# Loading a batch's max queries after its second key third, and half B's query DMAs split over three batches

## The chip, the cores and the metric

The kernel runs on one core of a Trainium2 chip. The metric is the device time of one execution in microseconds (us), as the median of several executions. The profiled execution is one further execution, taken by the hardware profiler.

## The reference, cut to what matters

Four transformer-like blocks run one after the other on `x` (16 batches of 56 rows, 128 wide) with a context of 1500 rows in each batch. Blocks 1, 2 and 3 each have a cross attention with 16 heads of 8 dimensions from the 56 rows to the 1500 context rows. That attention is where the change lies:

```python
q = (xq @ Wq + bq).reshape(B, Lq, nh, dh)
kv = (xkv @ Wkv + bkv).reshape(B, Lkv, 2, nh, dh)
k = kv[:, :, 0]
v = kv[:, :, 1]
scores = jnp.einsum('bqhd,bkhd->bhqk', q, k) / jnp.sqrt(jnp.float32(dh))
attn = jax.nn.softmax(scores, axis=-1)
out = jnp.einsum('bhqk,bkhd->bqhd', attn, v).reshape(B, Lq, H)
return x_q + (out @ Wp + bp)
```

Block 0 and the self attentions of blocks 2 and 3 stand outside the change.

## The kernel before, in words

Every engine has its own hand-written program, and the engines meet at semaphores. One cross attention ("layer" 1, 2 or 3 in the code) goes through its 16 batches with one call of `attend` for each batch, on every engine. `attend` gets `batch` (b), `following` (b+1), `behind` (b+2) and `third` (b+3).

TensorE (PE) does four things in `attend(b)`, woven together over twelve slots c = 0 to 11. It computes the scores of batch b, chunk by chunk (L1395). It computes the score maxima's input for batch b+1 in 24 "units" (L1343, function `unit`): unit 0 stands at c = 0 right behind the first chunk of scores, units 8 and 16 follow at about c = 4 and c = 7. It multiplies probabilities by values (L1369). And it prepares batch b+2: transposes of the context (L1208) at c = 1 to 3, its keys in three thirds of 500 columns (L1213) at c = 4, 6 and 8, then its values (L1219). Since PE works in order, unit 0 of batch b+1 stands ahead of everything else of `attend(b)` but the first chunk of scores.

The keys take a long way. ScalarE (ACT) evacuates a third to `k_full` (L878); GpSimd (POOL) splits it into two fp16 parts `k_hi` and `k_lo` (L698, L700); SyncE (SP) stores both parts to DRAM (`k_out`, L527, two DMAs) and loads them back in another layout as the tile `k_st` (`k_in`, L539, six DMAs). `k_in` waits for the landing of `k_out`. SP issues all of these DMAs, in the order in which its program is written, and waits in that order too.

The queries of all batches of a layer lie in `q_all`, and SP copies those of one batch at a time into two double-buffered tiles: `q_mx` for the units (function `q_max`) and `q_st` for the scores (function `q_scores`), both through `q_for` (L564). `unit` waits at u = 0 for `q_mx` of its batch and for the first key third:

```python
if u == 0:
    pe.wait_ge(sem(f"q_mx_loaded{p}"), 16 * (B // 2 * cr["n"] + i + 1))
    ...
if u % NP == 0:
    pe.wait_ge(sem(f"k_stacked{t}"), STACKED * (n + 1))
```

`q_all` is filled in two halves of eight batches. Half A is done in `first`, ahead of the layer. Half B (batches 8 to 15) is made while batches 4 to 6 run: VectorE (DVE) finishes the split queries in `attend(4)` at c = 6 (L1814), SP writes them to DRAM (`q_out`, L546, two DMAs of 224 KB) and reads them back in stacked form (`q_stack`, L555, six DMAs of 112 KB), and `q_ready` waits for their landing. SPLIT_BATCH is 4.

`load` (L480) fetches the context of batch b+4; it waits until the transposes of batch b+2 are done.

Of the kernel before, what the change touches and what calls it, by code (L numbers as in the profile page):

```python
# [32 lines left out]
ROWS = 2 + 3 * 2 * DH  # L33
# [148 lines left out]
SPLIT_BATCH = 4  # L182


def build(nc, x, cond, ctx, w, out, layers=4):

    with ExitStack() as stack:
        sems = {}

        def sem(name):  # L190
            if name not in sems:
                sems[name] = stack.enter_context(nc.semaphore(name))
            return sems[name]

        def sb(name, shape, dt=F32):
            return stack.enter_context(nc.sbuf_tensor(name, shape, dt))
# [11 lines left out]
        for name in WEIGHTS:  # L208
            if name not in FIRST_WEIGHTS:
                rows, cols = w[name].shape  # L210
# [4 lines left out]
        for name in VECTORS:  # L215
            place[name] = nv
            n = 1
# [64 lines left out]
        q_all = sb("q_all", [128, QUAD, B, PW], F16)  # L282
# [38 lines left out]
        def ge(eng, name, value=1):  # L321

            if not (isinstance(value, int) and value <= 0):
                eng.wait_ge(sem(name), value)
# [44 lines left out]
        def ge_known(eng, *waits):  # L369

            values = [(name, v if isinstance(v, int) else eng.to_reg(v)) for name, v in waits]
            eng.wait_ge(sem("ident_done"), 1)
            for name, v in values:
                ge(eng, name, v)
# [83 lines left out]
        def _(sp):  # L458
# [9 lines left out]
            def store_rows(u):  # L468
                ge(sp, *STEPS["cross", 3, u][-1].done)
                sp.dma_start(out.rearrange("b t d -> (b t) d")[u * HR:(u + 1) * HR].rearrange("(k p) d -> p k d", p=PW),  # L470
                             out_rows[u]).then_inc(sem("stored"), 16)

            for layer in range(layers):
# [8 lines left out]
                def load(batch):  # L482
                    b, i, p = batch

                    if layer == 1 and isinstance(b, int) and b < 2:
                        ge(sp, "ev_ready", B - 3 + b)
                        ge(sp, "bn_done", B - 3 + b)
                    else:
                        ge(sp, "cxT_ready", NT * (n0 + b - 1))
                    fetch(cx[:, p, :, :], b, f"cx_loaded{p}")  # L490
# [30 lines left out]
                def k_out(batch, t):  # L521

                    b, i, p = batch
                    n = n0 + b
                    ge_known(sp, (f"k_stacked{t}", STACKED * n), ("k_lo_done", NT * n + t + 1))
                    for part, src in enumerate((k_hi, k_lo)):
                        sp.dma_start(k_dram[part, :, TK * t:TK * t + TK], src[:, TK * t:TK * t + TK])\  # L527
                          .then_inc(sem(f"k_out{t}"), 16)

                def k_in(batch, t):  # L530

                    b, i, p = batch
                    n = n0 + b
                    free = 0 if isinstance(b, int) and b < 2 else 2 * C * (n - 2) + 2 * TC * (t + 1)
                    ge_known(sp, ("scores_ready", free), (f"k_out{t}", 32 * (n + 1)))
                    for a in range(2):
                        for k, part in enumerate(PARTS):
                            r = 64 * a + 2 + 2 * DH * k
                            sp.dma_start(k_st[r:r + 2 * DH, p, :, TK * t:TK * t + TK],  # L539
                                         k_dram[part, 64 * a:64 * a + 64, TK * t:TK * t + TK]  # L540
                                         .rearrange("(k d) s -> d k s", k=QUAD)).then_inc(sem(f"k_stacked{t}"), 16)

                def q_out(u):
                    ge(sp, "q_split", 2 * (layer - 1) + u + 1)
                    for part, src in enumerate((qh, ql)):
                        sp.dma_start(q_dram[part, :, HB * u:HB * u + HB, :], src.rearrange("p b h t -> p b (h t)"))\  # L546
                          .then_inc(sem("q_out"), 16)

                def q_stack(u):
                    lo, hi = HB * u, HB * u + HB  # L550
                    sp.wait_ge(sem("q_out"), 32 * (2 * (layer - 1) + u + 1))
                    for a in range(2):
                        for j, part in enumerate(Q_PART_OF):
                            r = 64 * a + 2 + 2 * DH * j
                            sp.dma_start(q_all[r:r + 2 * DH, :, lo:hi, :].rearrange("p k b n -> p k (b n)"),  # L555
                                         q_dram[part, 64 * a:64 * a + 64, lo:hi, :]
                                         .rearrange("(k d) b n -> d k (b n)", k=QUAD)).then_inc(sem("q_stacked"), 16)

                def q_ready(u):
                    sp.wait_ge(sem("q_stacked"), STACKED * (2 * (layer - 1) + u + 1))  # L560

                def q_for(batch, dst, name):
                    b, i, p = batch
                    sp.dma_start(dst[0:64 + ROWS, p, :, :], q_all[0:64 + ROWS, :, bass.ds(b, 1), :].rearrange("p k o n -> p k (o n)"))\  # L564
                      .then_inc(sem(f"{name}{p}"), 16)

                def q_scores(batch):

                    ge(sp, "scores_ready", 2 * C * (n0 + batch[0] - 1))
                    q_for(batch, q_st, "q_loaded")  # L570

                def q_max(batch):

                    ge(sp, "max_ready", UNITS * (n0 + batch[0] - 1))
                    q_for(batch, q_mx, "q_mx_loaded")
# [8 lines left out]
                def first():  # L584

                    load((0, 0, 0))
                    load((1, 0, 1))
                    keys_first(0)
                    if layer == 1:
                        keys_first(1)  # L590
                    for p in range(2):
                        ge(sp, f"q_loaded{p}", 16 * HB * (layer - 1))
                        ge(sp, f"q_mx_loaded{p}", 16 * HB * (layer - 1))
                    q_out(0)
                    q_stack(0)
                    q_ready(0)
                    q_max((0, 0, 0))
                    q_scores((0, 0, 0))
                    if layer > 1:
                        keys_first(1)  # L600
                    q_max((1, 0, 1))

                def attend(batch, following, behind, third):
                    b, i, p = batch
                    if following:
                        if b:
                            k_in(following, 2)
                        q_scores(following)
                    if b == SPLIT_BATCH + 2:
                        q_ready(1)  # L610
                    if behind:
                        q_max(behind)
                        if b + 4 < B:
                            load((b + 4, i + 2, p))
                        k_out(behind, 0)
                        k_in(behind, 0)
                        k_out(behind, 1)
                        k_in(behind, 1)
                        k_out(behind, 2)
                    if b == SPLIT_BATCH:  # L620
                        q_out(1)
                    if b == SPLIT_BATCH + 1:
                        q_stack(1)
                    if layer == 3 and b == B - 1:
                        store_rows(0)

                pipeline(first, attend)

            store_rows(1)
# [1364 lines left out]
```

## Time and profile before

| | |
|---|---|
| median of 3 runs | 1855.55 us (1852.5 to 1860.84) |
| the profiled execution's own time | 1839.58 us |
| its span | 1837.7 us, 50775 instructions |
| PE busy | 1594.1 us (87%) |
| DVE busy | 1137.7 us (62%) |
| ACT busy | 1029.5 us (56%) |
| POOL busy | 657.7 us (36%) |
| mean granted TensorE clock | 0.911 of full speed |
| chain that ended last | PE 64%, ACT 14%, DVE 10%, DMA 4%, issue 4%, SPq 2% |

The span is the time from the first to the last instruction in the profiled execution. Busy shares are averages over the whole span; the chain that ended last names what held up the end, followed backwards. SPq is SyncE's issuing of DMAs. The three cross attentions lie at about 339 to 740 us, 855 to 1273 us and 1398 to 1797 us of the span.

### The profile page before, as it was taken

The page shows a single profiled execution, that of the slowest core. Times are in us where ns is not written, and L with a number is a line of the kernel's source. Part 1 is how long each engine was busy: PE and PEld are TensorE (multiplying, and loading weights), DVE is VectorE, ACT ScalarE, POOL GpSimd, SP SyncE. Part 2 cuts the span into 40 slices and gives each one's busy share as a digit, 9 for nine tenths or more (in the row PEclk, how much of TensorE's full clock was granted, in tenths as well). Part 3 has the DMA queues.
Part 4 walks back from the last instruction along what each step waited for, and adds up shares of the span by engine and source line. Part 5 has one row for each costly group of instructions (what it writes and reads, how often), then busy time and mean ns, then how long its engine had stood idle before and what let it go on. Part 6 is the DMA issues. An engine that isn't in the chain of part 4 may idle for free.

```text
span 1837.7 us, 50775 instructions
## 1 busy us (share of the span) xinstructions
PE 1594.1 (87%) x20495; PEld 1001.1 (54%) x20495; DVE 1137.7 (62%) x2324; ACT 1029.5 (56%) x1942; POOL 657.7 (36%) x898
## 2 busy tenths in 40 slices
PE   6888877599999998887999999987877999999985
PEld 4556533266655566443666666655433666666553
DVE  4555353577767675456777767673456777676651
ACT  2334232286767776332777767763523777677662
POOL 4000326066655545245456655411141222122100
PEclk9999899599999998886999999987897999999985
DMA  7222022144454432024444544320024445444310
GB/s 198 68 67 84 17 59 59 37 124 120 126 139 117 128 90 80 1 60 96 109 119 135 135 128 119 99 79 2 1 59 99 126 124 144 130 121 122 83 43 6
DMA packets 180243, 167.69 MB, mean 91 GB/s; under 512 B 67215, under 2 KB 171602, under 8 KB 180018
## 3 DMA queue, kind: packets, MB, share of 16 engines
q1 hardware_dynamic: 178434, 163.45, 34.6%
q8 instruction: 161, 2.64, 0.6%
q10 hardware_dynamic: 1008, 1.05, 0.2%
q14 instruction: 64, 0.52, 0.1%
q0 software_dynamic: 576, 0.02, 0.0%
HBM read 114.46 MB, written 40.08 MB: 84 GB/s over the span
## 4 chain that ended last, share of the span: by engine, by line
PE 64%; ACT 14%; DVE 10%; DMA 4%; issue 4%; SPq 2%; POOL 1%; ACTq 0%; DVEq 0%; POOLq 0%
PE PS L1369 13%; PE PS L1219 8%; PE PS L1395 7%; PE PS L1213 7%; PE PS L1343 4%; ACT q_parts L971 4%; DVE mx L1827 3%; PE PS L1208 3%; PE PS L1050 3%; PE PS L1134 3%; PE PS L1472 2%; PE PS L1154 2%; ACT v_sb L882 2%; ACT cxT L873 2%; PE PS L1125 2%
## 5 line engine op out<-in xcount | busy, mean ns | idle before, releaser
L1827 DVE TENSOR_REDUCE mx<-PS 112x1 f32<-112x500 f32 x1152 | 715.5, 671 | 243.4 <-PE PS L1343 240.1
L971 ACT ACTIVATE q_parts<-PS 125x448 f32<-125x448 f32 x1152 | 562.9, 545 | 149.1 <-PE PS L1395 145.1
L698 POOL CAST k_hi<-k_full 128x500 f16<-128x500 f32 x144 | 89.1, 619 | 664.2 <-issue 564.2
L733 POOL TENSOR_SCALAR cx<-cx,norm_b 125x128 f32<-125x128 f32 x384 | 302.9, 813 | 33.4 <-issue 17.7
L1395 PEld LDWEIGHTS PS<-q_st,k_st 50*125 50x125 f16 x4608 | 186.1, 139 | 224.2 <-ACT q_parts L971 152.5
L1395 PE MATMUL PS<-q_st,k_st 50*125 50x112 f16 x4608 | 261.9, 235 | 37.8 <-ACT q_parts L971 28.8
L1369 PE MATMUL PS<-q_parts,v_sb 125*18 125x112 f32 x9216 | 294.1, 271 | 0.0
L1343 PE MATMUL PS<-k_st,q_mx 50*112 50x500 f16 x1152 | 264.0, 402 | 33.8 <-DMA q_mx<-q_all 18.2
L1369 PEld LDWEIGHTS PS<-q_parts,v_sb 125*18 125x18 f32 x9216 | 220.0, 101 | 55.5 <-issue 43.1
L700 POOL TENSOR_TENSOR k_lo<-k_full,k_hi 128x500 f16<-128x500 f32 x144 | 163.9, 1138 | 21.6 <-POOL k_hi L698 4.0
L882 ACT ACTIVATE v_sb<-PS 125x512 f32<-125x512 f32 x144 | 87.0, 604 | 100.2 <-PE PS L1219 100.1
L1343 PEld LDWEIGHTS PS<-k_st,q_mx 50*112 50x112 f16 x1152 | 93.0, 133 | 74.1 <-DVE mx L1827 34.3
L878 ACT ACTIVATE k_full<-PS,vec 128x500 f32<-128x500 f32 x144 | 97.5, 677 | 55.5 <-PE PS L1213 55.5
L1208 PE MATMUL PS<-ident,cx 125*128 125x125 f32 x576 | 96.7, 292 | 25.3 <-ACT cxT L870 11.3
L1208 PEld LDWEIGHTS PS<-ident,cx 125*128 125x128 f32 x576 | 62.3, 145 | 62.3 <-ACT v_sb L882 18.1
L956 ACT ACTIVATE q_st<-PS 2x448 f16<-2x448 f32 x48 | 25.7, 535 | 97.0 <-PE PS L1354 95.6
L675 POOL COPY A_first<-A 128x56 f32<-128x56 f32 x32 | 7.5, 233 | 183.0 <-PE PS L1472 106.3
L993 ACT ACTIVATE A<-A 56x896 f32<-56x896 f32 x32 | 30.4, 950 | 71.5 <-DVE A L1925 71.4
L1472 PE MATMUL PS<-first_w,A_first 128*56 128x448 f32 x128 | 70.3, 638 | 0.0
L827 ACT ACTIVATE A_first<-PS,neg 56x1500 f32<-56x1500 f32 x16 | 24.1, 1506 | 82.2 <-DVE neg L1642 82.2
L1922 DVE TENSOR_REDUCE s_mx<-PS 56x16 f32<-56x896 f32 x32 | 34.6, 1082 | 57.1 <-PE PS L1472 57.1
L873 ACT ACTIVATE cxT<-PS 128x500 f32<-128x500 f32 x96 | 57.5, 599 | 19.8 <-PE PS L1208 19.7
(278 smaller groups left out, 2026.6 us busy)
## 6 DMA issues: line engine op xcount, KB each, us to landing
k_st<-k_dram SPq DMA_DIRECT2D x864, 62.5 KB, 2.2
cx<-in_ctx SPq DMA_DIRECT2D x56, 672.0 KB
k_dram<-k_hi SPq DMA_DIRECT2D x144, 125.0 KB, 1.9
k_dram<-k_lo SPq DMA_DIRECT2D x144, 125.0 KB, 2.0
v_sb<-in_ctx SPq DMA_DIRECT2D x8, 672.0 KB
q_mx<-q_all SPq DMA_DIRECT2D x48, 99.8 KB
q_st<-q_all SPq DMA_DIRECT2D x48, 99.8 KB
cx<-in_ctx SPq DMA_DIRECT2D x56, 78.0 KB
```

Source lines behind the costliest of these rows:

```text
L700: pool.tensor_tensor(k_lo[:, cols], k_full[:, p, cols], k_hi[:, cols], ALU.subtract)\
L733: last = pool.tensor_scalar(cx[:, p, c, :], cx[:, p, c, :], norm_b[:, p, 0, c:c + 1], norm_b[:, p, 1, c:c + 1], ALU.subtract, ALU.mult)
L882: act.activation(v_sb[:, p, TC * t:TC * t + TC, :, 0:2 * DH], PS[0:KC, bank, :].rearrange("p (c r d) -> p c r d", c=TC, r=NP), ACT.Copy)\
L971: act.activation(probs[:, c % RING, u * HR:(u + 1) * HR], PS[0:KC, (2 * c + u) % SC_RING, 0:HR], ACT.Exp).then_inc(sem("exp_done"), 1)
L1208: last = pe.transpose(PS[:, bank, c * KC:(c + 1) * KC], cx[:, p, TC * t + c, :], ident[0:KC, 0:KC])
L1213: mm(PS[:, bank, 0:TK], cr["kw"], cxT[:, TK * t:TK * t + TK], start=True, stop=True)\
L1219: last = mm(PS[0:KC, bank, c * D:(c + 1) * D], cxT[:, k0:k0 + KC], cr["vw"], start=True, stop=True)
L1343: mm(PS[0:PW, MX_BANK + u % MX_RING, 0:TK], q_mx[64 * a:64 * a + ROWS, p, k, :], k_st[64 * a:64 * a + ROWS, p, k, TK * t:TK * t + TK], sta ...
L1369: last = mm(PS[32 * j:32 * j + VW, PV_BANK, k * PW:k * PW + PW], v_sb[:, p, c, r, :], probs[:, c % RING, r * PW:r * PW + PW], start=(c == ...
L1395: last = mm(PS[0:KC, (2 * c + a) % SC_RING, k * PW:k * PW + PW], k_st[64 * a:64 * a + ROWS, p, k, c * KC:(c + 1) * KC], q_st[64 * a:64 * a ...
L1472: last = mm(PS[0:T, 2 * p + u, 0:HR], q_b[:, p, :], km_b[:, p, NP * u:NP * u + NP, :].rearrange("p h t -> p (h t)"), start=True, stop=True)
L1827: dve.tensor_reduce(mx[:, r, t:t + 1], PS[0:PW, MX_BANK + u % MX_RING, 0:TK], AX.X, ALU.max)\
```

## The change

In `attend` on SyncE the load of `q_mx` for batch b+2 moves from ahead of the context load and the first key third to behind `k_in(behind, 1)`, for every batch. `q_out(1)` moves from the end of `attend(4)` to behind `k_in(behind, 0)` there. `q_stack(1)` no longer runs in one piece at the end of `attend(5)`: three of its DMAs run behind `k_in(behind, 0)` in `attend(5)`, the other three at the same place in `attend(6)`. `q_ready(1)` moves down in front of `q_max` in `attend(6)`. The tiles `q_mx` and `q_st` are loaded with all 128 partitions instead of 114.

```diff
-                def q_stack(u):
+                def q_stack(u, rows=(0, 1)):
                     lo, hi = HB * u, HB * u + HB
                     sp.wait_ge(sem("q_out"), 32 * (2 * (layer - 1) + u + 1))
-                    for a in range(2):
+                    for a in rows:
...
                     b, i, p = batch
-                    sp.dma_start(dst[0:64 + ROWS, p, :, :], q_all[0:64 + ROWS, :, bass.ds(b, 1), :].rearrange("p k o n -> p k (o n)"))\
+                    sp.dma_start(dst[:, p, :, :], q_all[:, :, b, :])\
                       .then_inc(sem(f"{name}{p}"), 16)
...
                         q_scores(following)
-                    if b == SPLIT_BATCH + 2:
-                        q_ready(1)
                     if behind:
-                        q_max(behind)
                         if b + 4 < B:
                             load((b + 4, i + 2, p))
                         k_out(behind, 0)
                         k_in(behind, 0)
+                        if b == SPLIT_BATCH:
+                            q_out(1)
+                        if b == SPLIT_BATCH + 1:
+                            q_stack(1, (0,))
+                        if b == SPLIT_BATCH + 2:
+                            q_stack(1, (1,))
                         k_out(behind, 1)
                         k_in(behind, 1)
+                        if b == SPLIT_BATCH + 2:
+                            q_ready(1)
+                        q_max(behind)
                         k_out(behind, 2)
-                    if b == SPLIT_BATCH:
-                        q_out(1)
-                    if b == SPLIT_BATCH + 1:
-                        q_stack(1)
```

SyncE's program for one batch in the middle of a layer, before. The first `k_st` row is the last key third of batch b+1; the rows behind `cx` belong to batch b+2:

```order
L539 DMA k_st<-k_dram 16x4x500 x6
L564 DMA q_st<-q_all 114x4x112
L564 DMA q_mx<-q_all 114x4x112
L480 DMA cx<-in_ctx 112x1536
L480 DMA cx<-in_ctx 13x1536
L527 DMA k_dram<-k_hi 128x500
L527 DMA k_dram<-k_lo 128x500
L539 DMA k_st<-k_dram 16x4x500 x6
L527 DMA k_dram<-k_hi 128x500
L527 DMA k_dram<-k_lo 128x500
L539 DMA k_st<-k_dram 16x4x500 x6
```

The same stretch of SyncE's program in the changed kernel:

```order
L539 DMA k_st<-k_dram 16x4x500 x6
L564 DMA q_st<-q_all 128x4x112
L480 DMA cx<-in_ctx 112x1536
L480 DMA cx<-in_ctx 13x1536
L527 DMA k_dram<-k_hi 128x500
L527 DMA k_dram<-k_lo 128x500
L539 DMA k_st<-k_dram 16x4x500 x6
L527 DMA k_dram<-k_hi 128x500
L527 DMA k_dram<-k_lo 128x500
L539 DMA k_st<-k_dram 16x4x500 x6
L564 DMA q_mx<-q_all 128x4x112
```

The load of `q_mx` for batch b+2 has moved past the context load, two key stores of two DMAs each, and two key loads of six DMAs each, with the waits that stand ahead of them.

SyncE's program in `attend(5)` of the changed kernel, from its context load on; in the kernel before, all six `q_all` DMAs stood behind the third pair of key stores:

```order
L480 DMA cx<-in_ctx 112x1536
L480 DMA cx<-in_ctx 13x1536
L527 DMA k_dram<-k_hi 128x500
L527 DMA k_dram<-k_lo 128x500
L539 DMA k_st<-k_dram 16x4x500 x6
L555 DMA q_all<-q_dram 16x4x896 x3
L527 DMA k_dram<-k_hi 128x500
L527 DMA k_dram<-k_lo 128x500
L539 DMA k_st<-k_dram 16x4x500 x6
L564 DMA q_mx<-q_all 128x4x112
```

Three of the `q_all` DMAs now stand ahead of the second key third, and the other three stand at the same place one batch later.

## Rows read from the trace of the kernel before

**Rows 1.** The page's busy part: engine, busy us, share of the span, instructions.

```profile
PE 1594.1 (87%) x20495; PEld 1001.1 (54%) x20495; DVE 1137.7 (62%) x2324; ACT 1029.5 (56%) x1942; POOL 657.7 (36%) x898
```

**Rows 2.** Waits of PE: us in total, times, longest.

```profile
PE PS L1343 <- DMA q_mx<-q_all: 18.2, 3, 14.9
PE PS L1343 <- DMA k_st<-k_dram: 10.0, 7, 2.9
```

**Rows 3.** Timeline (start, us): first units of batches 1, 15; stretches between such (us first).

```profile
356.69 0.66 PE L1343 MATMUL PS<-k_st,q_mx 50*112 50x500 f16 x2
...
699.21 0.41 PE L1343 MATMUL PS<-k_st,q_mx 50*112 50x500 f16 x2
...
356.70:699.20 342.50, 320.68 (x5165) 212.31 (x5164) 249.29 (x447) 249.13 (x487) 190.70 (x268) 0.98 0.45 116
...
sum 1031.70, PE 975.40 PEld 641.24 DVE 747.06 ACT 741.70 POOL 453.19; mean PE 325.13 PEld 213.75 DVE 249.02 ACT 247.23 POOL 151.06
```

**Rows 4.** Timeline, layer 1: first units of batches 12 and 13, SP's DMAs between.

```profile
629.60 0.51 PE L1343 MATMUL PS<-k_st,q_mx 50*112 50x500 f16 x2
...
641.25 0.43 SPq L527 DMA_DIRECT2D k_dram<-k_lo  x1
643.16 3.40 SPq L539 DMA_DIRECT2D k_st<-k_dram  x6
...
647.08 0.43 SPq L527 DMA_DIRECT2D k_dram<-k_lo  x1
649.11 2.66 SPq L539 DMA_DIRECT2D k_st<-k_dram  x6
...
654.04 0.41 PE L1343 MATMUL PS<-k_st,q_mx 50*112 50x500 f16 x2
```

**Rows 5.** Timeline, layer 1: batch 9's first unit and SP's first two key thirds.

```profile
541.71 0.43 SPq L527 DMA_DIRECT2D k_dram<-k_lo  x1
547.00 2.68 SPq L539 DMA_DIRECT2D k_st<-k_dram  x6
...
552.52 0.42 PE L1343 MATMUL PS<-k_st,q_mx 50*112 50x500 f16 x2 [0.21 <-DMA k_st<-k_dram]
...
553.16 2.66 SPq L539 DMA_DIRECT2D k_st<-k_dram  x6
```

**Rows 6.** Timeline: half B's stacking and the unit behind it in layer 1, a like unit in layer 3.

```profile
508.21 2.81 SPq L555 DMA_DIRECT2D q_all<-q_dram  x6
...
511.12 2.70 SPq L539 DMA_DIRECT2D k_st<-k_dram  x6
...
517.25 0.41 PE L1343 MATMUL PS<-k_st,q_mx 50*112 50x500 f16 x1 [2.88 <-DMA k_st<-k_dram]
...
1566.21 0.66 PE L1343 MATMUL PS<-k_st,q_mx 50*112 50x500 f16 x1 [2.72 <-DMA k_st<-k_dram]
```

**Rows 7.** Stretches: us, busy by engine, granted PE clock, DMA share, GB/s.

```profile
517.60:521.00 3.40, 3.40 (x44) 2.30 (x44) 1.32 (x3) 0.98 (x2) 0.00 (x0) 0.50 1.00 280
...
1063.80:1070.50 6.70, 6.64 (x66) 4.52 (x64) 4.04 (x7) 4.17 (x9) 0.91 (x2) 0.50 0.50 125
...
602.20:606.00 3.80, 3.37 (x35) 2.30 (x36) 3.32 (x7) 2.28 (x6) 3.80 (x6) 1.00 0.37 84
```

**Rows 8.** Timeline: two waits of first units, and a key store after one.

```profile
602.22 0.42 PE L1343 MATMUL PS<-k_st,q_mx 50*112 50x500 f16 x2 [1.04 <-DMA k_st<-k_dram]
...
1061.85 0.42 PE L1343 MATMUL PS<-k_st,q_mx 50*112 50x500 f16 x2 [2.10 <-DMA k_st<-k_dram]
...
1075.37 0.35 SPq L527 DMA_DIRECT2D k_dram<-k_hi  x1
```

**Rows 9.** DMA issues of the page: count, KB each, median us to landing.

```profile
k_st<-k_dram SPq DMA_DIRECT2D x864, 62.5 KB, 2.2
k_dram<-k_lo SPq DMA_DIRECT2D x144, 125.0 KB, 2.0
```

**Rows 10.** Chain that ended last, layer 1's start: the q_mx load's issue to landing.

```profile
336.00 3.13 DMA q_mx<-q_all
```

## The prediction

> **What bounds the kernel now.** I read the busy part first: PE is busy 87% of the span, the next engine 62% [rows 1], so a batch costs what PE's row of work costs unless PE is made to wait. The list of waits says how often that happens: only small sums, of which 10.0 us go to `k_st` loads and 18.2 us to `q_mx` loads. 14.9 of the 18.2 are one wait, at layer 1's start, behind the stacking of half A [rows 2]. So inside a layer PE never waits for `q_mx` today. The timeline of PE then gives the period. From batch 1's first unit to batch 15's are 14 periods, 342.5 us in layer 1, and 1031.7 us for the 42 of the three layers [rows 3], 24.6 us each. They are not equal. Batches without an extra step of the row-wise chain take about 22 us, those with many steps 27 to 30. I read all 42 of them between the first and last units in the same way; the sum below uses how they are spread.
>
> The timeline with SP's DMAs beside PE's units shows where a `q_mx` load would stand. Batch 12's first unit starts at 629.60, and batch 13's keys are made behind it. SP stores third 0 until 641.68, loads it back from 643.16, stores third 1 until 647.51, loads it back from 649.11 to 651.77, and batch 13's first unit starts at 654.04 [rows 4]. That is 22.2 us from one first unit to the end of the next batch's second `k_in`. Where SP lags, it is later still: batch 9's first unit starts at 552.52, and the second key third of that very batch is issued only by 555.82 [rows 5].
>
> **The change part by part.**
>
> *The `q_mx` load moves behind the second key third.* The load for batch b+2 is needed by unit 0 in PE's `attend(b+1)`, and everything else of that `attend` is queued behind this unit on PE. Before, it had a whole period in hand. Now it is issued when `k_in(b+2, 1)` ends. For batch 13 that is 651.77 plus landing against a unit at 654.04: about level. For batch 9 it is 555.82 plus landing against 552.52: late by over 3 us before the landing is counted. Among the 42 batches only 6 have 2.5 us or more between that end and their first unit.
>
> The load is tied to PE itself, since the keys it stands behind are made behind the previous first unit. So this is a loop with a period of its own: D, from a first unit to the end of the next batch's second `k_in`, plus L, from there to the landing. For D I take 22.5 us. In batches where SP does not lag, as in [rows 4] with 22.2, I read 21.6 to 23.9. The longer ones (up to 30.8) come from SP's lag, where a context load is issued just ahead of the key store, and SP can go on only 5.3 us behind the start of that store [rows 5]. That lag goes, because PE is held back until SP is ahead. For L: with 114 partitions a load took 3.13 us [rows 10]; a `k_st` load has 2.2 as its median, and a store from all 128 partitions 2.0 [rows 9]. The new load has 128 partitions but more bytes than `k_st`; I take 2.5, between them and nearer the short rows. The floor of a period is then 25.0 us, with 21.6 + 2.2 = 23.8 and 23.7 + 3.1 = 26.8 as ends.
>
> Of the 42 periods, 29 are shorter than 25.0, by 52.6 us together. Raising them to the floor and taking out the `k_st` waits within them (9.4 us, nearly the 10.0 of [rows 2]) gives **+43 us**. With 24.2 as floor it would be +22, with 26.2 +81.
>
> [...]
>
> *Half B's stacking.* Before, its six DMAs stood ahead of the third `k_in`: 2.81 us of issue, the key loads then only at 511.12, and PE waited 2.88 us; in layer 3 the like wait was 2.72 [rows 6]. Both are in the 9.4 above. Now half of it, 1.4 us of issue, stands in `attend(5)` and half in `attend(6)`, and `q_out` with some 0.9 us of issue in `attend(4)`, all ahead of `k_out(1)` and therefore inside D. Each also puts 336 or 448 KB ahead of the key store in the queue; I add 0.3 and 1.4 us for that. With 2.3 + 1.7 + 1.7 on the floor of three batches in each layer this is **+16 us**. Lower end nothing, if the store's landing hides it. `q_ready` costs nothing: its DMAs have the two waits of the second third to land.
>
> *TensorE's clock.* [...] After the 2.10 us wait at 1061.85 it was 0.50 from 1063.8 to 1070.5, and the next key store came 13.5 us after that first unit, where the one at 641.25 came 11.7 us after its own. After the 1.04 us wait it stayed at 1.00 [rows 4, 6, 7, 8]. So a wait of about 2 us or more is followed by 3.4 to 6.8 us at half clock, and these lie between the first unit and the first key third, which is inside D. Some 17 of the periods are short enough (below 23.3) that they would wait 1.7 us or more. At 2.2 us each that is 37, less some 7 for the three old waits that go: **+30 us**. Ends: nothing, and +60 if nearly every batch waits that long.
>
> *The rest.* At each layer's start the `q_mx` load is on the path [rows 10]: 0.7 us less, three times, **-2 us**. With the load out of the way, context load and first key store go out 0.8 us sooner. That is worth nothing where PE waits for the load behind them.
>
> Sum: 43 + 16 + 30 - 2 = +87. I take +80, since after a wait ACT and DVE have caught up and PE runs a little freer. The profiled execution took 1839.6 us, 16 below the median of the runs; the sum is made on its trace and laid on the median: 1855.6 + 80 = **1935 us**.
>
> **The rivals.**
>
> *The loop holds, but the clock doesn't fall and D sits at its short end.* Then a floor of 24.2 gives +22, up to +43 with some of the split: 1872 to 1900. For it: D was 21.6 to 22.2 in several batches without a lag. Against it: the half clock followed waits of this size in the rows that I have. Chance 0.22.
>
> *Faster: the load lands in time.* If SP gets so far ahead that `k_in(b+2, 1)` ends 2.5 us before the first unit, only the savings stay: 9.4 us of `k_st` waits, 7 for the clock, 2 at the starts, so 1837. It decides at D + L below the natural period, 22 us for the short batches. Against it: the keys' way alone (K matmul, evacuation, split, store, landing, load) is in D, and its shortest is 21.6. Chance 0.04.
>
> *No change that can be measured:* floor at 23.6 or less and no clock loss, +10 or less, 1855 to 1865. Chance 0.06.
>
> *Much slower.* If the clock stays at half for most of a layer, D grows as in layer 1's first batch at low clock, by 4 us or so: 42 times 4 on top of +59 is over 200 us, 2000 and more. Chance 0.08.
>
> The forecast itself, 1900 to 1985, has 0.60.
>
> **How the numbers follow.** Faster or slower by over 0.5%, 9 us, is about what a measurement of this kernel can tell from no change. Faster 0.04, same 0.06, slower 0.90. The range of 1872 to 1985 holds the forecast and the short-end rival, 0.82 together.
>
> **What would show it.** In the changed profile: a wait of PE at L1345, two lines further down than now, for `q_mx<-q_all`, some 30 to 42 times and of 1 to 4 us each, near 80 us in total on PE and its weight loads; no wait for `k_st` to speak of; periods of 25 us or more from first unit to first unit, and longest around batches 6 to 8; SP's first key store 11 to 13.5 us behind the first unit; stretches of half clock right behind the first units; the q loads shorter from issue to landing. I am wrong in mechanism if PE waits for `q_mx` in fewer than ten batches, and in size if D turns out 1 us off (about 25 us of the total) or the clock holds.

## The result, and the profile after

The changed kernel takes 2005.9 us as median (1994.4 to 2018.4) against 1855.3 us (1852.5 to 1860.8) before. The ratio is 1.081, with a 95% interval of 1.076 to 1.085: 150 us or 8% slower. Slower was forecast, but by 80 us, to 1935, and to 1985 at most.

The busy part of the page after the change (engine, busy us, share of the span, instructions), where PE stood at 1594.1 us [rows 1]:

```profile
PE 1699.9 (84%) x20495; PEld 1070.2 (53%) x20495; DVE 1140.7 (57%) x2324; ACT 1039.7 (52%) x1942; POOL 660.0 (33%) x898
```

PE has the same 20495 matmuls and is busy 105.8 us longer with them. So a good part of the loss isn't waiting at all: PE works slower. PE's list of waits (us in total, times, longest) begins with the wait that was forecast:

```profile
PE PS L1345 <- DMA q_mx<-q_all: 106.9, 32, 14.3
PE PS L1397 <- ACT q_parts L973: 28.2, 46, 1.9
```

Before, `q_mx` had 18.2 us in 3 waits [rows 2]. The 14.3 is still the one at layer 1's start, and one more, of 3.05 us, stands at layer 2's start. The other 30, of 0.3 to 6.9 us and 89.6 us together, are new and stand at the first units of batches 2 to 15. The wait for `k_st`, 10.0 us before, is gone from the list.

The same stretches as in [rows 3], from batch 1's first unit to batch 15's in each layer (us, busy time of each engine, granted PE clock, DMA share, GB/s), and their sum:

```profile
369.30:763.90 394.60, 351.24 (x5168) 232.73 (x5164) 250.38 (x447) 252.99 (x489) 190.94 (x268) 0.89 0.39 103
942.90:1343.20 400.30, 357.75 (x5183) 234.78 (x5180) 252.47 (x451) 251.95 (x494) 189.55 (x253) 0.90 0.38 102
1538.70:1935.60 396.90, 353.92 (x5164) 232.99 (x5161) 247.01 (x444) 248.09 (x489) 73.33 (x84) 0.89 0.39 102
sum 1191.80, PE 1062.91 PEld 700.50 DVE 749.86 ACT 753.02 POOL 453.83; mean PE 354.30 PEld 233.50 DVE 249.95 ACT 251.01 POOL 151.28
```

The 42 periods grew from 1031.7 to 1191.8 us, +160.1. PE's busy time in them grew from 975.4 to 1062.9, **+87.5**, and its idle time (sum less busy) from 56.3 to 128.9, **+72.6**. The two terms are the whole 160. They are somewhat large for a usual execution: the profiled execution of the kernel before was 16 us under its median, that of the changed kernel 12.5 us above its own. The granted clock of layer 1's stretch fell from 0.98 to 0.89; over all 42 periods the trace's record of the granted clock has 252 us at half clock, where it had 49. Batch 9 of layer 1, the batch of [rows 5], in the timeline of PE and SP's queue (start, us, engine, line; in brackets the idle time before it and what ended it):

```profile
566.93 0.73 PE L1345 MATMUL PS<-k_st,q_mx 50*112 50x500 f16 x2 [3.42 <-DMA q_mx<-q_all]
...
582.48 0.44 SPq L527 DMA_DIRECT2D k_dram<-k_lo  x1
584.42 3.02 SPq L539 DMA_DIRECT2D k_st<-k_dram  x6
...
587.96 0.43 SPq L527 DMA_DIRECT2D k_dram<-k_lo  x1
589.89 3.69 SPq L539 DMA_DIRECT2D k_st<-k_dram  x6
593.63 0.60 SPq L564 DMA_DIRECT2D q_mx<-q_all  x1
...
596.02 0.42 PE L1345 MATMUL PS<-k_st,q_mx 50*112 50x500 f16 x2 [2.88 <-DMA q_mx<-q_all]
```

This is the loop. Batch 8's first unit starts at 566.93 after a wait. The keys made behind it leave SP's queue by 593.58, the `q_mx` load goes out at 593.63, and PE gets on with batch 9 at 596.02, 2.4 us later, after another wait: a period of 29.1 us. Two stretches, one behind this first unit and one behind a first unit that had not waited, show why it is 29 and not 25:

```profile
568.00:578.00 10.00, 9.90 (x92) 6.83 (x91) 5.33 (x11) 5.50 (x10) 0.00 (x0) 0.55 0.21 52
...
451.80:461.00 9.20, 8.51 (x122) 5.41 (x121) 6.92 (x13) 7.81 (x16) 4.30 (x6) 1.00 0.41 105
```

Behind 566.93 the mean clock was 0.55 for 10 us, so nearly all of it was at half clock (the clock record has 0.50 from 566.83 to 577.07), and SP's second DMA of the first key store came 15.6 us behind the first unit. At batch 4 of layer 1, which had not waited, the clock was 1.00, and its period ended with a wait of the same size:

```profile
451.81 0.53 PE L1345 MATMUL PS<-k_st,q_mx 50*112 50x500 f16 x2
...
463.48 0.80 SPq L527 DMA_DIRECT2D k_dram<-k_lo  x1
...
477.56 0.42 PE L1345 MATMUL PS<-k_st,q_mx 50*112 50x500 f16 x2 [3.40 <-DMA q_mx<-q_all]
```

The key store's second DMA came 11.7 us behind the first unit, as in [rows 4], and the period was 25.8 us. Five periods of the changed kernel kept the full clock up to their first key store and ended in a wait for `q_mx`: they took 24.7 to 25.9 us.

### The profile page after: what moved, and what is told of

The parts are those of the page before. It is cut to its first block and busy times, and to the rows that moved or that the text cites. A ratio compares the mean times of both kernels' runs of the same rounds, so it can differ in the third digit from the quotient of the medians.

```text
span 2016.6 us, 50775 instructions
## 1 busy us (share of the span) xinstructions
PE 1699.9 (84%) x20495; PEld 1070.2 (53%) x20495; DVE 1140.7 (57%) x2324; ACT 1039.7 (52%) x1942; POOL 660.0 (33%) x898
## 5 line engine op out<-in xcount | busy, mean ns | idle before, releaser
L1345 PE MATMUL PS<-k_st,q_mx 50*112 50x500 f16 x1152 | 283.5, 441 | 112.9 <-DMA q_mx<-q_all 106.9
L1397 PEld LDWEIGHTS PS<-q_st,k_st 50*125 50x125 f16 x4608 | 199.9, 149 | 233.4 <-ACT q_parts L973 158.8
L735 POOL TENSOR_SCALAR cx<-cx,norm_b 125x128 f32<-125x128 f32 x384 | 304.9, 809 | 35.3 <-issue 18.1
L1371 PE MATMUL PS<-q_parts,v_sb 125*18 125x112 f32 x9216 | 313.0, 283 | 0.0
L1397 PE MATMUL PS<-q_st,k_st 50*125 50x112 f16 x4608 | 278.7, 246 | 36.8 <-ACT q_parts L973 28.2
L1371 PEld LDWEIGHTS PS<-q_parts,v_sb 125*18 125x18 f32 x9216 | 233.4, 106 | 63.1 <-issue 48.1
L1345 PEld LDWEIGHTS PS<-k_st,q_mx 50*112 50x112 f16 x1152 | 98.3, 144 | 154.9 <-DMA q_mx<-q_all 93.5
L1210 PE MATMUL PS<-ident,cx 125*128 125x125 f32 x576 | 118.4, 341 | 20.1 <-ACT cxT L872 9.1
L1210 PEld LDWEIGHTS PS<-ident,cx 125*128 125x128 f32 x576 | 77.5, 172 | 65.5 <-ACT v_sb L884 18.6
L1641 DVE TENSOR_REDUCE neg<-PS 56x1 f32<-56x1500 f32 x16 | 27.4, 1711 | 73.7 <-PE PS L1136 73.6
L1221 PE MATMUL PS<-L_xcond_ca_vw,cxT 128*125 128x128 f32 x384 | 63.7, 317 | 4.9 <-ACT k_full L880 1.7
```

What stands on the lines that cost most here:

```text
L735: last = pool.tensor_scalar(cx[:, p, c, :], cx[:, p, c, :], norm_b[:, p, 0, c:c + 1], norm_b[:, p, 1, c:c + 1], ALU.subtract, ALU.mult)
L1210: last = pe.transpose(PS[:, bank, c * KC:(c + 1) * KC], cx[:, p, TC * t + c, :], ident[0:KC, 0:KC])
L1221: last = mm(PS[0:KC, bank, c * D:(c + 1) * D], cxT[:, k0:k0 + KC], cr["vw"], start=True, stop=True)
L1345: mm(PS[0:PW, MX_BANK + u % MX_RING, 0:TK], q_mx[64 * a:64 * a + ROWS, p, k, :], k_st[64 * a:64 * a + ROWS, p, k, TK * t:TK * t + TK], sta ...
L1371: last = mm(PS[32 * j:32 * j + VW, PV_BANK, k * PW:k * PW + PW], v_sb[:, p, c, r, :], probs[:, c % RING, r * PW:r * PW + PW], start=(c == ...
L1397: last = mm(PS[0:KC, (2 * c + a) % SC_RING, k * PW:k * PW + PW], k_st[64 * a:64 * a + ROWS, p, k, c * KC:(c + 1) * KC], q_st[64 * a:64 * a ...
```

## The experiments

Each ratio is to the kernel before on the same chip. Where the text below speaks of periods, it means the 42 from batch 1's first unit to batch 15's in each layer, as above.

**The moved load alone.** In the kernel before:

```diff
                     if behind:
-                        q_max(behind)
...
                         k_in(behind, 1)
+                        q_max(behind)
                         k_out(behind, 2)
```

> The kernel before, with the load of q_mx for batch b+2 moved behind the second key third, and nothing else of the change (114 partitions, half B's DMAs where they were). Theory 1 (the moved load is the whole loss): it stands behind the same keys, lands about 0.7 us later in each of 42 periods than with 128 partitions, so it is as slow as the changed kernel, 1990 to 2040 us, with 30 or more waits of PE for q_mx and over 200 us of half clock inside the periods. Theory 2 (half B's DMAs ahead of the second key third are a good part of it): at most 1950 us.

Measured: 2011.1 us, ratio 1.081 (1.074 to 1.089), the same as the whole change. PE's first wait:

```profile
PE PS L1343 <- DMA q_mx<-q_all: 108.5, 35, 15.0
```

Its stretches:

```profile
sum 1179.50, PE 1048.81 PEld 692.30 DVE 748.63 ACT 751.22 POOL 451.79; mean PE 349.60 PEld 230.77 DVE 249.54 ACT 250.41 POOL 150.60
```

Theory 1 holds: the moved load, with 114 partitions, is enough for a loss of this size, with 217 us of half clock in the periods. That it is the same 8% as the whole change is in part chance. The changed kernel has a faster load and half B's DMAs in the loop besides, and the run with all partitions below tells these two apart.

**The moved load taken back.** In the changed kernel:

```diff
                     if behind:
+                        if b != SPLIT_BATCH + 2:
+                            q_max(behind)
...
                             q_ready(1)
-                        q_max(behind)
+                            q_max(behind)
```

> The changed kernel with the load of q_mx back at the top of attend, except in attend(6), where half B is not yet stacked and it stays behind the second key third. Theory 1: the loss goes; one late load in each layer remains, at 5 to 10 us each with its half clock, so 1850 to 1880 us. Theory 2: 1900 us or more, since the DMAs of half B still stand inside the keys' way in three batches of each layer.

Measured: 1871.2 us, ratio 1.003 (0.9997 to 1.006). Nearly the whole loss is gone, and the waits that are left are the one at layer 1's start and the one late load in each layer:

```profile
PE PS L1347 <- DMA q_mx<-q_all: 35.3, 4, 14.2
...
PE PS L1347 <- DMA k_st<-k_dram: 6.9, 5, 1.6
```

Three waits of 7 us each on average are 21 of the 35.3. So the spread DMAs of half B cost little where the `q_mx` load isn't behind them. How little isn't settled, since this kernel also has the 128 partitions, which by themselves gave 0.7% (below).

**Work in the place of the wait.** PE gets matmuls to do ahead of its wait for `q_mx`, into a PSUM bank that unit 0 overwrites. In the changed kernel:

```diff
                     if u == 0:
-                        pe.wait_ge(sem(f"q_mx_loaded{p}"), 16 * (B // 2 * cr["n"] + i + 1))
                         ge(pe, "shift_done", n)
                         ge(pe, "shift_done1", n)
+                        if b > 1:
+                            ge(pe, "max_done", UNITS * n + 1 - MX_RING)
+                            for _ in range(9):
+                                mm(PS[:, MX_BANK, 0:PW], ident[:, :], ident[:, 0:PW], start=True, stop=True)
+                        pe.wait_ge(sem(f"q_mx_loaded{p}"), 16 * (B // 2 * cr["n"] + i + 1))
```

> The changed kernel, with nine matmuls of 128x128 by 112 columns, whose result is overwritten, on PE ahead of its wait for q_mx at unit 0 of batches 2 to 15, some 2 us of work each. The output is unchanged. Theory A (the wait costs twice, once as a wait and once as half clock behind it): waits shrink by about the matmuls' time, most half clock inside the periods goes (from 252 us to under 100), the first key store comes again 11 to 12 us behind the first unit, and the kernel gets 40 to 80 us faster, 1925 to 1965 us, though it does more. Theory B (the low clock is a bystander, since PE waits anyway): the time stays within 1% or grows, 1995 to 2040 us.

Measured: 1974.7 us, ratio 1.060 (1.053 to 1.067), clear of the changed kernel's 1.081 (1.076 to 1.085). By ratio this is 38 us faster, with 378 matmuls more. The time lies between the two theories, 10 us above the 1965 of theory A and 20 below the 1995 of theory B; the gain of 38 is just below the 40 that theory A asked for. Its stretches:

```profile
366.90:754.40 387.50, 359.09 (x5417) 246.87 (x5414) 248.78 (x447) 250.71 (x489) 190.89 (x268) 0.96 0.41 105
929.10:1320.10 391.00, 362.50 (x5434) 245.77 (x5430) 251.41 (x451) 249.54 (x496) 188.86 (x252) 0.97 0.41 105
1512.30:1891.30 379.00, 356.02 (x5419) 243.14 (x5416) 245.74 (x444) 245.46 (x491) 73.35 (x84) 0.98 0.42 108
sum 1157.50, PE 1077.61 PEld 735.79 DVE 745.93 ACT 745.70 POOL 453.10; mean PE 359.20 PEld 245.26 DVE 248.64 ACT 248.57 POOL 151.03
```

The clock is back at 0.96 to 0.98, and half clock in the periods fell from 252 to 67 us, as theory A had it. PE's waits for `q_mx` fell from 106.9 to 48.4 us. What the matmuls themselves take is read from their control.

**The control: the same matmuls in the kernel before**, where there is no wait to fill.

> The kernel before, with the same nine matmuls ahead of unit 0 of batches 2 to 15, a control for their own price. PE bounds that kernel, so they cost their time in nearly each of 42 batches: 42 times 2 us, 1920 to 1945 us by either theory. If they cost less than 40 us there, PE has slack at this place that the argument of the prediction denied.

Measured: 1941.8 us, ratio 1.042 (1.035 to 1.049), 75 to 79 us for 42 batches, as expected of a kernel that PE bounds. The sum of its stretches:

```profile
sum 1120.40, PE 1074.41 PEld 733.78 DVE 745.28 ACT 745.26 POOL 453.09; mean PE 358.14 PEld 244.59 DVE 248.43 ACT 248.42 POOL 151.03
```

PE's busy time is 99.0 us above the 975.4 of [rows 3], 0.26 us for each of 378 matmuls. In the changed kernel with them it was 1077.6: without the 99.0, 978.6, against 1062.9 where PE only waited. So keeping PE at work took back 84 of the 87.5 us that the low clock had cost. (The busy time of the matmuls' own line is 94.8 us in both kernels; taken off instead, it gives 80.) The net gain is smaller because the matmuls are work too: 99 us of them went in, 84 us of slow work and 49 us of idle time came out, and the periods are 34 us shorter.

**Only in the short batches.** Edit: `if b > 4 and b not in (11, 12, 13, 14)` in place of `if b > 1`.

> The changed kernel with the nine matmuls only ahead of unit 0 of batches 5 to 10 and 15, the short periods in which the loop makes PE wait. Theory A (the half clock is a cost of its own): without the price in the long batches, 15 to 40 us faster than with the matmuls in all 14 batches, so 1935 to 1960 us, though waits in the other batches bring some half clock back. Theory B (the matmuls only take the place of idle time): 1975 us or more.

Measured: 1970.0 us, ratio 1.060 (1.052 to 1.067), the same as with all of them. My figure was a miss: the price saved in the long batches came back in those that now waited unfilled. Its PE busy time in the periods was 1059.8, of which 189 matmuls of 0.26 us are 49, so some 35 us of slow work remained, where 3 had remained with all of them. Its periods, 1156.1 us in all, hold 96.3 us of idle time against 79.9. So of the 49 us saved 32 came back as slow work and 16 as idle time.

**Five matmuls instead of nine.** Edit: `range(5)`.

> The changed kernel with five matmuls instead of nine ahead of PE's wait at unit 0 of batches 2 to 15, 1.1 to 1.2 us of work. Theory A: waits of 2.5 to 3 us shrink below 2, and most half clock goes (under 130 us in the periods), at half the price in the batches without a wait, so 1945 to 1975 us. Theory B (little depends on the clock): 1990 to 2015 us with as much half clock as in the changed kernel.

Measured: 1998.8 us, ratio 1.075 (1.066 to 1.084). This can't be told from the changed kernel, and the expected time was a miss. The sum of its stretches says why:

```profile
sum 1180.40, PE 1082.19 PEld 725.99 DVE 748.11 ACT 750.71 POOL 453.06; mean PE 360.73 PEld 242.00 DVE 249.37 ACT 250.24 POOL 151.02
```

PE's 1082.2 less 210 matmuls of 0.26 us, 55, is 1027: still 52 us above 975.4 (by the busy time of the matmuls' own line, 57, it is 49). Half clock in the periods was 165 us, where theory A wanted less than 130. With half the work in the waits, more than half of the clock's cost stayed.

**The load ahead of the second key load.** In the changed kernel it moves up past one call, `k_in(behind, 1)`, which is a wait for the store's landing and six DMAs:

```diff
                         k_out(behind, 1)
-                        k_in(behind, 1)
                         if b == SPLIT_BATCH + 2:
                             q_ready(1)
                         q_max(behind)
+                        k_in(behind, 1)
```

> The changed kernel with the q_mx load two steps earlier: behind the second key store, ahead of the second key load, so in the landing of that store. Theory 1 (a loop from first unit to first unit through the moved load): the way to its issue is 5 to 6 us shorter, 17 us, and with 2.5 us of landing 19.5 to 20 us lies under every natural period of 22 us. No loop wait is left outside batches 6 to 8, and the time is that of the kernel before within 1%, 1845 to 1880 us. A rival (any late place of the load costs): over 1900 us.

Measured: 1856.4 us, ratio 0.9985 (0.995 to 1.002). One position in SP's program, and the 8% are gone. In the periods whose first key store came at full clock the load was now issued from 16.8 us behind the first unit on, where it had been 21.5 at the least. Seven waits for `q_mx` are left inside the layers, 13 us in all, at batches 7 to 10. That a late place costs as such is refuted.

**The load behind the third key store.** In the changed kernel:

```diff
-                        q_max(behind)
                         k_out(behind, 2)
+                        q_max(behind)
```

> The changed kernel with the q_mx load one step later, behind the third key store, whose issue takes 0.8 to 0.9 us. Theory 1 (a loop through the moved load, in most of 42 periods): 0.85 us more in each, and a little more half clock, so 30 to 50 us slower than the changed kernel, ratio to before 1.095 to 1.110. A rival (PE waits for the keys' landing anyway, and the q_mx load is only the last to arrive): within 10 us of the changed kernel, ratio 1.076 to 1.087.

Measured: 2051.8 us, ratio 1.103 (1.095 to 1.111), some 40 us more for 0.85 us of issue. PE's first wait and the sum of the stretches:

```profile
PE PS L1345 <- DMA q_mx<-q_all: 136.0, 36, 14.3
```

```profile
sum 1225.10, PE 1065.00 PEld 702.47 DVE 750.25 ACT 754.05 POOL 453.66; mean PE 355.00 PEld 234.16 DVE 250.08 ACT 251.35 POOL 151.22
```

The periods grew by 33.3 us, 31.2 of it idle time (160.1 against 128.9). Of the 36 waits 35 lie inside the layers, and 0.85 us in 35 periods would be 30. So the load sits in a loop that is run through in most of the batches. The rival, that PE waits for the keys' landing anyway, is refuted.

**The moved load with all partitions, half B left alone.** Edit: the moved load as in the first experiment, and the changed `q_for`.

> The kernel before, with the q_mx load moved behind the second key third and both q tiles loaded with 128 partitions; half B's DMAs stand where they were. So it is the changed kernel without the spreading of half B, and the earlier run with 114 partitions with only the partitions changed. Theory 1: the load lands 0.7 us sooner in about 30 loop periods than with 114, and half B's 2 us in each of three periods per layer are out of the loop: 15 to 40 us faster than either, ratio 1.060 to 1.073. A rival (the clock decides, since the waits remain at 2 to 3 us, and takes back what the terms give): ratio 1.076 or more.

Measured: 1983.4 us, ratio 1.069 (1.063 to 1.076). The sum of its stretches:

```profile
sum 1159.60, PE 1042.90 PEld 686.25 DVE 749.71 ACT 751.69 POOL 451.92; mean PE 347.63 PEld 228.75 DVE 249.90 ACT 250.56 POOL 150.64
```

Against the changed kernel the periods are 32.2 us shorter: what half B's DMAs cost once they stand inside the loop, 12 of it as idle time and 20 as slow work. By the ratios, 1.069 against 1.081, it is 21 us; the changed kernel's profiled execution was its slowest, so the smaller figure is the safer one. Against the same edit with 114 partitions (periods 1179.5 us) they are 19.9 shorter, which goes to the faster loads; the two times are 1.069 and 1.081, with intervals that just overlap. So the moved load and the partitions together make 6.9% of the 8.1%, and half B's DMAs the rest.

**All partitions alone.** The kernel before with the changed `q_for`.

> The kernel before, with q_mx and q_st loaded with all 128 partitions and nothing else. Theory 1: about 0.8 us sooner landed per load and 0.15 us less issue; on the path at three layer starts and where SP lags, so -3 to -12 us, ratio 0.993 to 0.999. A rival: the 56 more packets per load cost as much as the better spread gives, ratio 1.000.

Measured: 1849.5 us, ratio 0.993 (0.990 to 0.997). The page of the changed kernel gives the median landing of these loads:

```profile
q_mx<-q_all SPq DMA_DIRECT2D x48, 112.0 KB, 2.3
```

In this run's own chain, at layer 1's start, the load took 2.38 us from issue to landing:

```profile
350.84 2.38 DMA q_mx<-q_all
```

With 114 partitions it was 3.13 at the same place [rows 10]. This part of the change is a gain by itself, hidden under the loss.

**A version from the findings.** The `q_mx` load goes where SP waits anyway, half B's stacking behind key stores of `attend(5)`, `q_out` back to its place. Only the lines put in are shown; the same calls go from their places in the changed kernel:

```diff
                         k_out(behind, 0)
+                        if b == SPLIT_BATCH + 2:
+                            q_ready(1)
+                        q_max(behind)
                         k_in(behind, 0)
...
                         k_out(behind, 1)
+                        if b == SPLIT_BATCH + 1:
+                            q_stack(1, (0,))
                         k_in(behind, 1)
...
                         k_out(behind, 2)
+                        if b == SPLIT_BATCH:
+                            q_out(1)
+                        if b == SPLIT_BATCH + 1:
+                            q_stack(1, (1,))
```

> A version made from the findings: all 128 partitions; the q_mx load behind the first key store, where SP waits over 2 us for the landing anyway; half B's stacking in halves behind the second and the third key store of attend(5); q_out where it was before. Theory 1: 0.8 us less of SP's row per batch, so the k_st waits of 9.4 us and the 2 to 3 us waits with their half clock go: 10 to 25 us faster than before, ratio 0.987 to 0.995. A rival (DMA queues, not SP's issue, delay the keys): ratio 0.998 to 1.003, with the k_st waits still there.

Measured: 1842.2 us, ratio 0.991 (0.987 to 0.995), faster than both kernels. PE's waits:

```profile
PE PS L1345 <- DMA q_mx<-q_all: 14.4, 1, 14.4
...
PE PS L1345 <- DMA k_st<-k_dram: 3.2, 2, 2.5
```

No wait for `q_mx` is left inside a layer, and `k_st` has 3.2 us instead of 10.0 [rows 2]. How much of the gain is the order and how much the partitions isn't settled: 0.991 and 0.993 have intervals that overlap.

## Why the prediction was right in kind and wrong in size

**The loop.** Right. The load behind the second key third makes PE wait in most batches, it carries most of the loss, and one call earlier or later moves the time as a loop would. Where the clock held, as in the period of 25.8 us above, the floor of 25.0 was 0.8 short; the five such periods took 24.7 to 25.9. L was taken as 2.5 us. In the median of the 42 loads it was 2.35, though eleven took 3.0 to 4.1, so that the mean was 2.6.

**Its size in waiting.** The steps gave 43 + 16 us for the floor and half B's DMAs. PE's idle time in the periods grew by 72.6. The 14 us too many may belong to the clock, since a slow PE also makes the keys later, and PE waits for what stands behind them. No run separates them.

**Half B's DMAs inside the loop.** Forecast +16; the run without them was 21 us faster by the ratios, and in the profiles 32 us shorter in its periods, 12 in idle time and 20 in slow work. The issue and queue terms together were about right, though the queue's 0.3 and 1.4 us were estimates that no run shows by themselves, and the clock was left out of them.

**TensorE's clock.** This is the step that failed. It read: "Some 17 of the periods are short enough (below 23.3) that they would wait 1.7 us or more. At 2.2 us each that is 37, less some 7 for the three old waits that go: +30 us." PE's busy time for the same matmuls grew by 87.5 us in the periods, and by 105.8 in the whole span. Two things were mis-sized, the number of slow starts and the price of one. I counted 17 batches at 2.2 us each. In the changed kernel's clock record 28 of the 42 periods have half clock between their first unit and their first key store. Three of them are the first of a layer, as before; the other 25 follow a wait. The 87.5 us over these 25 are 3.5 us each. I had taken 3.4 to 6.8 us of half clock from the old waits, the 3.4 from the stretch at 0.50 behind the 2.88 us wait [rows 6, 7]; of the 25, 12 had 9 to 10 us, as in the stretch at 568. My comparison of the key stores was also uneven: 13.5 us was the first DMA of its pair [rows 8], and 11.7 us the second [rows 4]. Second against second the delay was 2.3 us, not 1.8.

The count failed because I set it by the natural period. Of the 25, 10 came at the end of a period that before the change, without its waits for keys, had been 23.3 us or longer, and 8 of these 10 periods had themselves begun at half clock. Behind a slow start the first key store comes up to 4 us later (15.2 instead of 11.2 us), so D grows, so PE waits again at the next first unit even in a batch that would have been long enough: the wait feeds itself. The rival "much slower" named that growth of D, at 2000 us and more, with a chance of 0.08. What came lies at its edge.

The filled waits show that this is cause and not company. With work in the place of the wait PE's own work took 978.6 us again instead of 1062.9, and the kernel got 38 us faster though it did more. In the trace half clock follows most waits and not all: of the 29 waits for `q_mx` that stand at the head of one of the 42 periods, 25 were followed by half clock before the first key store. The other four, of 0.30, 0.38, 1.67 and 2.73 us, were not.

**Partitions.** The traces show what the 128 partitions changed. With 114 the semaphore of each of the 48 loads of `q_mx` got one early increment (1.2 us behind the issue in the median) and six later ones, the last at 3.1 us; with 128 it got sixteen, the last at 2.35 us. The loads are also spread wider: while the packets of one `q_mx` load and hardly any others ran, the mean busy share of the core's 16 DMA engines was 0.44 with 114 partitions (99 GB/s, the kernel before, from 354.60 to 355.60 us) and 1.01 with 128 (223 GB/s, all partitions alone, from 368.55 to 369.05 us).

**The sum.** In the profiled pair the span grew by 178.9 us, 160.1 of it in the periods, where 43 + 16 + 30 had been forecast. The rest, 18.8, is nearly all more busy time of PE outside them (105.8 less 87.5 is 18.3). Most of that seems to be spread between executions and not the change: outside the periods PE was busy for 618.7 us before and 637.0 after, but also for 632.3 us in the version from the findings and for 629.3 in the control, whose PE has no new waits for `q_mx`. The medians differ by 150.6. The cut from 87 to 80 for engines that catch up has nothing in the runs to support it.

## What to carry to other kernels

Before a transfer is moved down a queue, read what stands between its new place and the engine that waits for it. If that engine's own earlier work is in the chain, it is a loop, and its length is compared with the natural period in every round, not with a share of busy time. And when a wait is added to every round on TensorE, give the lower clock behind it a price of its own, and let the slower rounds count towards the next wait. Here the waits were 3 us on average, 73 us more of idle time in all, and the work at the lower clock cost 87 us beside them.

## What the runs showed of the hardware that I had not expected

A wait of 3.4 us on PE was followed by 10 us at a mean clock of 0.55, though PE was busy for 9.9 of these 10 us. The length of the wait alone doesn't tell: one of 1.24 us was followed by 6.8 us of half clock, and one of 2.73 us by none. Nine matmuls of 0.26 us ahead of the wait took back nearly all of the slow work (80 to 84 of 87.5 us), while five left some 50 us of it. And a 112 KB copy of 512 rows of 224 bytes over 128 partitions landed in 2.4 us, where 456 such rows over 114 partitions had taken 3.13.
